# Scatters of edge records paced by the dense part that runs beside them

## Chip, cores and metric

The kernel runs on one core of a Trainium2 chip. The metric is the device time of one execution in microseconds; the median of the timed runs counts. The profile is of one separate execution.

## Reference

Two layers of a graph network, each a graph part and a feed-forward part with residual sums, over N = 6250 nodes of 256 features and E = 100,000 edges:

```python
x = x + L0_gnn(layernorm(x), src, dst, edge_weight, w_self, w_neigh)   # weighted sums of gathered rows, two products, rows divided by their norm
x = x + L0_ffn(layernorm(x), ...)   # shared MLP plus 4 experts, the best 2 weighted
x = x + L1_gnn(layernorm(x), (src, dst), edge_attr_64, ...)
x = x + L1_ffn(layernorm(x), ...)   # 8 experts, the best 2 weighted
...
def L1_gnn(x, edge_index, edge_attr, u, batch, W1, b1, W2, b2):
    src = edge_index[0]
    sums = segment_sum(edge_attr, src, n)          # 64 attributes of each edge, summed by node
    counts = segment_sum(ones, src, n)
    combined = concatenate([x, sums / maximum(counts, 1)[:, None], u[batch]], axis=1)
    return relu(combined @ W1 + b1) @ W2 + b2
```

What matters here is that the second graph part sums 100,000 edge records (64 attributes and two more words, 264 bytes) by source node, for which the kernel first sorts them, and that this sorting needs nothing of the first layer's dense work.

## The kernel before

The nodes lie in 49 tiles of 128 rows, in NG = 7 groups of G = 7 tiles, resident in SBUF. The work has four stages, each a block with one program for each engine; engines meet only at semaphores and at the ends of blocks.

**Gathers.** POOL gathers the normalised source rows of 128 edges with one indirect DMA (L343, 784 of them); ACT multiplies them by the edge weights, TensorE (PE) adds them into tiles by one-hot products, VectorE (DVE) makes the one-hots and adds the results to `acc`. Beside this DVE ranks the edges by source, so that each edge has its place in the sorted list (`pos_i`). At the end of the stage POOL issues the first BEGUN = 16 scatters (L356).

**Dense part and scatters.** This is the stage that the change touches. PE, DVE and ACT go through the 7 groups, each as two chains of 4 and 3 tiles (`CHAINS`) whose steps alternate: the products of the first graph part, the first feed-forward part, and the first product of the second graph part. All of it is written out, without loops on the chip. ACT evicts each product from PSUM: in `ffn` six times at L957 and three at L960, in `part_out` four times at L977; with two chains and seven groups that makes 182 evictions. The first eviction of a group comes after the graph part's products, the squares and norms (L931), a normalisation, the turn of the rows (PE L1078, DVE L1233) and the gate's logits (PE L1092, L1094). The first group can't begin before its weights have landed, which SP loads at the start of the block.

Meanwhile POOL scatters the other 768 columns of 128 edge records to their sorted places in DRAM (`sorted_edges`, L904), one indirect DMA for each column c. The records come through a stage of two halves of SC = 28 columns, which SP refills (L862) once the half's scatters have landed. POOL waits for a half to be loaded, and before every second scatter (EACH = 2) for the landing of the batch that lies two batches back (TURNS = 2). After its scatters POOL has only seven short additions left in this block (L914).

**Edge part.** After the dense part ACT loads the sorted records in 340 items, DVE makes one-hots (L1330), PE multiplies (L1177), DVE adds (L1339). The records are sorted in three segments of columns, and ACT waits before each segment for the landing of its scatters alone:

```python
SEGMENTS = ((0, 448), (448, 672), (672, NC))
...
for n in range(len(SEGMENTS)):
    for turn in range(TURNS):
        act.wait_ge(s_sca[turn], LANDED[n][turn])
    with act.Fori(ITS4_FROM[n], (ITS4_FROM + (ITS4,))[n + 1]) as it:
        loads(it)
```

The segments have 160, 104 and 76 items; the loop goes by 16 items, so the wait for the last segment stands before item 256. The last stage holds the rest of the second layer.

Of the kernel before, what the change touches and what calls it, by code (L numbers as in the profile page):

```python
# [15 lines left out]
NC = -(-E // (P * RUN)) * RUN  # L16
# [91 lines left out]
PHASES = len(CHAINS) * NG  # L108
# [6 lines left out]
EACH = 2  # L115
# [3 lines left out]
BEGUN = 16  # L119
# [3 lines left out]
def build(nc, a, out):  # L123
# [5 lines left out]
    def sem(name):  # L129
        return ctx.enter_context(nc.semaphore(name))  # L130
    def dram(name, shape, dt=f32):
        return nc.dram_tensor(name, shape, dt, kind="Internal").ap()
    with ctx:
# [79 lines left out]
        if True:  # L213
# [66 lines left out]
            with nc.Block() as block:  # L280
                @block.sync
                def _(sp):
                    sp.dma_start(dst_i[:, :], a["dst"].rearrange("(p c) -> p c", p=P)).then_inc(s_dst, 16)
                    sp.dma_start(raw_i[:, 0, :, :], a["src"].rearrange("(j q e) -> q j e", q=QC, e=P)).then_inc(s_cols, 16)
                    for n, (g0, g1) in enumerate(X_PARTS):
                        sp.dma_start(xr[:, g0 * G:g1 * G, :],
                                     a["x"][g0 * G * P:g1 * G * P, :].rearrange("(t p) d -> p t d", p=P)).then_inc(s_x[n], 16)
                    sp.dma_start(raw_i[:, 1, :, :], a["dst"].rearrange("(j q e) -> q j e", q=QC, e=P)).then_inc(s_cols2, 16)
                    sp.dma_start(raw_f[:, 2, :, :], a["w"].rearrange("(j q e) -> q j e", q=QC, e=P)).then_inc(s_cols2, 16)
                    sp.dma_start(src_i[:, :], a["src"].rearrange("(p c) -> p c", p=P)).then_inc(s_src, 16)  # L290
                    for g in range(NG):
                        for h, tiles in enumerate(XN_PARTS):
                            sp.wait_ge(s_xn[h], (g + 1) * len(tiles))
                            first = (g * G + tiles[0]) * P
                            sp.dma_start(xn_d[first:first + len(tiles) * P, :].rearrange("(t p) d -> p t d", p=P),
                                         xn_st[:, tiles[0]:tiles[-1] + 1, :]).then_inc(s_xst[h], 16)
                    sp.wait_ge(s_rank, 1)
                    for h in range(2):
                        sp.dma_start(stage[:, h, :, :], a["attr"].rearrange("(p c) f -> p c f", p=P)[:, h * SC:(h + 1) * SC, :]).then_inc(s_att[h], 16)
                    sp.wait_ge(s_row, 2)  # L300
                    sp.dma_start(item_d.unsqueeze(0), row4_i[:, :, :]).then_inc(s_rst, 16)
                    sp.wait_ge(s_rst, 16)
# [399 lines left out]
        if True:  # L702
# [30 lines left out]
            def nth(c, g):  # L733
                return len(CHAINS) * g + c
            def tiles_to(c, g):
                return G * g + c * len(CHAINS[0])
            def span(c):
                return slice(CHAINS[c][0], CHAINS[c][-1] + 1)
            def columns(c):
                return slice(CHAINS[c][0] * P, (CHAINS[c][-1] + 1) * P)  # L740
# [88 lines left out]
            s_y3 = sem("l0_ffn_products")  # L829
            s_x2 = sem("l0_rows_done")  # L830
            s_hxo = [sem(f"l1_part_out{c}") for c in range(len(CHAINS))]
            with nc.Block() as block:
                @block.sync
                def _(sp):
# [48 lines left out]
                @block.gpsimd  # L883
                def _(pool):
                    own = Chain(pool, s_c3)
                    own.add(pool.iota(rev_i[:, :], pattern=[[-1, 8]], base=8, channel_multiplier=0))
                    own.add(pool.memset(pair[:, :, :], 0.0))
                    own.add(pool.memset(cf[:, :, 4:5], 1.0))
                    own.sync()
                    for m in range(4):  # L890
                        own.add(pool.affine_select(out=pair[:, m // 2, m % 2 * (P // 2):(m % 2 + 1) * (P // 2)],
                                                   in_=pair[:, m // 2, m % 2 * (P // 2):(m % 2 + 1) * (P // 2)],
                                                   compare_op=ALU.not_equal, fill=1.0, base=-m,
                                                   pattern=[[0, P // 2]], channel_multiplier=1))
                    own.sync()
                    for c in range(BEGUN, NC):
                        q, batch = c // SC, c // EACH
                        turn = batch % TURNS
                        if c % SC == 0:
                            pool.wait_ge(s_att[q % 2], (q // 2 + 1) * 16)  # L900
                        if c % EACH == 0:
                            if batch >= TURNS:
                                pool.wait_ge(s_sca[turn], batch // TURNS * (16 * EACH))
                        pool.indirect_dma_start(  # L904
                            out=edges_d, out_offset=bass.IndirectOffsetOnAxis(ap=pos_i[:, c:c + 1], axis=0),
                            in_=stage[:, q % 2, c % SC, :], in_offset=None).then_inc(s_sca[turn], 16)
                    for turn in range(TURNS):
                        pool.wait_ge(s_sca[turn], 16 * EACH * PER_TURN * (NC // SC // 2))
                    for c in range(len(CHAINS)):
                        pool.wait_ge(s_hxo[c], NG * 16)  # L910
                    pool.wait_ge(s_w3, 16 * (18 + 8))
                    for g in range(NG):
                        x = xr[:, g * G:(g + 1) * G, :]
                        pool.tensor_tensor(x, x, gb2[:, :].unsqueeze(1).to_broadcast([P, G, D]), ALU.add).then_inc(s_c5, 1)  # L914
                @block.scalar
                def _(act):
# [18 lines left out]
                    def deviation3(c, g):  # L935
                        act.wait_ge(s_v3, nth(c, g) + 1)
                        nc.scalar.activation(ln["sd"][:, span(c)], ln["mv"][:, span(c), 1], ACT.Sqrt, bias=eps[:, :]).then_inc(s_sd3, 1)
# [8 lines left out]
                    def ffn(c, g):  # L946
                        w = len(CHAINS[c]) * P
                        act.wait_ge(s_mx, nth(c, g) + 1)
                        nc.scalar.activation(gt["e"][:, span(c), :], gt["l"][:, span(c), :], ACT.Exp).then_inc(s_ex, 1)
                        if g:  # L950
                            act.wait_ge(s_hxo[c], g * 16)
                        for m in range(6):
                            if m == 5:
                                act.wait_ge(s_df, nth(c, g) + 1)
                                nc.scalar.activation(g1["x"][:, span(c)], g1["d"][:, span(c)], ACT.Exp).then_inc(s_ex2, 1)
                            act.wait_ge(s_h1, nth(c, g) * 6 + m + 1)
                            nc.scalar.activation(h1[:, m, columns(c)], psum[:, 4 * c + m % 3, 0:w], ACT.Relu, bias=b1[:, m:m + 1]).then_inc(s_h1c, 1)  # L957
                        for m in range(3):
                            act.wait_ge(s_h2, nth(c, g) * 3 + m + 1)
                            nc.scalar.activation(h2[:, m, columns(c)], psum[:, 4 * c + m, 0:w], ACT.Relu, bias=b2[:, m:m + 1]).then_inc(s_h2c, 1)  # L960
                    def deviation4(c, g):
                        act.wait_ge(s_v6, nth(c, g) + 1)
                        nc.scalar.activation(ln["sd"][:, span(c)], ln["mv"][:, span(c), 1], ACT.Sqrt, bias=eps[:, :]).then_inc(s_sd6, 1)
# [7 lines left out]
                    def part_out(c, g, deviation):  # L971
                        w = len(CHAINS[c]) * P
                        for m in range(4):
                            if m == 2 and deviation:
                                deviation3(c, g + 1)
                            act.wait_ge(s_h5, nth(c, g) * 4 + m + 1)
                            nc.scalar.activation(h1[:, m, columns(c)], psum[:, 4 * c + m % 2, 0:w], ACT.Copy).then_inc(s_hc5, 1)  # L977
                        act.wait_ge(s_hc5, nth(c, g) * 4 + 4)
                        act.dma_start(hx_d[g * P:(g + 1) * P, :].rearrange("p (m n) -> p m n", m=4)[:, :, columns(c)],
                                      h1[:, 0:4, columns(c)]).then_inc(s_hxo[c], 16)  # L980
# [1151 lines left out]
```

## Time and profile before

| | us |
|---|---|
| timed runs, median of 3 (lowest, highest) | 3212.76 (3200.77, 3222.05) |
| span of the profiled execution | 4237.5 |
| time of the profiled execution beside its span | not recorded |

The profiled execution is one execution with the recording on; its span runs from its first to its last instruction. It is longer than the timed runs, which are made without it. Busy time of the profiled execution: PE 2615.1 us (62% of the span), DVE 1421.8 (34%), ACT 974.8 (23%), POOL 1860.1 (44%). Times in the rows below are microseconds from the start of the span. "Idle before" is the time that an engine stood still before an instruction, with what ended it: an instruction of another engine, a DMA, "remote" (a semaphore event for which the trace has no source on this core) or "issue" (nothing that the profile shows).

### The profile page before, as it was taken

What the parts mean: (1) busy time and instruction counts of PE and PEld (TensorE: products, weight loads), DVE (VectorE), ACT (ScalarE), POOL (GpSimd) and SP (SyncE); (2) the same over time, 40 slices, a digit from 0 to 9 for tenths busy, and PEclk for the clock granted to TensorE, in tenths of its full rate; (3) what the DMA queues carried; (4) which work ended last, traced back from release to release, by engine and by line L of the source; (5) the groups of instructions that cost most, each with busy time, mean ns of one, the idle gap of its engine ahead of it and who ended that gap; (6) DMA issues with size and microseconds to landing.
All of it is one profiled execution on the core that took longest, in us unless ns stands there. A gap on an engine that the chain in (4) does not pass through costs nothing. (4 is left out here: it accounts for less than half of the span.)

```text
span 4237.5 us, 48325 instructions
## 1 busy us (share of the span) xinstructions
PE 2615.1 (62%) x11859; PEld 2002.8 (47%) x11860; DVE 1421.8 (34%) x3597; ACT 974.8 (23%) x2337; POOL 1860.1 (44%) x1901
## 2 busy tenths in 40 slices
PE   0445545556554221111211699998999879999998
PEld 0333334434443010100100466657996567888898
DVE  5211225666621000000000244438995542222222
ACT  4555222222220000000000244430003421111122
POOL 4566665665665777777777100002000342222222
PEclk9767667676776555555555799999998889999999
DMA  6223333332232111111111000006553454444455
GB/s 187 80 87 91 88 87 97 87 89 80 85 85 62 52 45 51 52 52 62 42 51 42 24 18 18 35 18 172 146 146 116 162 153 110 111 117 116 106 148 148
DMA packets 217917, 372.80 MB, mean 88 GB/s; under 512 B 48901, under 2 KB 146542, under 8 KB 216815
## 3 DMA queue, kind: packets, MB, share of 16 engines
q0 software_dynamic: 82928, 157.51, 14.4%
q1 hardware_dynamic: 77100, 154.03, 11.1%
q10 hardware_dynamic: 57812, 60.35, 5.0%
q8 instruction: 34, 0.56, 0.1%
q14 instruction: 43, 0.35, 0.0%
HBM read 290.03 MB, written 81.71 MB: 88 GB/s over the span
## 5 line engine op out<-in xcount | busy, mean ns | idle before, releaser
L673 PE MATMUL psum<-arena 128*128 x1984 | 632.1, 481 | 514.1 <-issue 325.7
L343 POOL DMA_INDIRECT arena<-xn_rows,arena x784 | 749.7, 956 | 449.7 <-issue 241.9
L904 POOL DMA_INDIRECT sorted_edges<-arena x768 | 766.7, 998 | 284.3 <-issue 265.1
L673 PEld LDWEIGHTS psum<-arena 128*128 128x128 f32 x1984 | 463.3, 243 | 683.1 <-issue 605.6
L408 ACT ACTIVATE arena<-arena 128x256 f32<-128x256 f32 x784 | 338.1, 496 | 697.3 <-DMA arena<-xn_rows,arena 642.6
L1177 PE MATMUL psum<-arena,acc 128*65 128x128 f32 x2720 | 311.9, 275 | 23.8 <-DVE arena L1330 23.8
L1177 PEld LDWEIGHTS psum<-arena,acc 128*65 128x65 f32 x2720 | 296.0, 138 | 40.1 <-DVE arena L1330 32.0
L1103 PE MATMUL psum<-arena 128*128 128x512 f32 (+1 forms) x336 | 172.3, 669 | 229.4 <-ACT arena L957 133.2
L1796 PE MATMUL psum<-arena,xr 128*128 x1344 | 301.7, 382 | 13.7 <-DVE xr L2021 9.1
L1783 PE MATMUL psum<-xr 128*128 128x256 f32 x1344 | 299.1, 381 | 1.0 <-DVE xr L2015 1.0
L575 DVE TENSOR_TENSOR acc<-acc,psum 128x256 f32 x248 | 103.0, 415 | 550.4 <-remote 366.8
L1796 PEld LDWEIGHTS psum<-arena,xr 128*128 128x128 f32 x1344 | 253.8, 192 | 49.1 <-issue 16.0
L1783 PEld LDWEIGHTS psum<-xr 128*128 128x128 f32 x1344 | 256.8, 191 | 36.6 <-DVE xr L2015 1.4
L1330 DVE SCALAR_TENSOR_TENSOR arena<-psum,acc 128x512 f32<-128x512 f32 x340 | 252.5, 744 | 25.2 <-PE psum L1177 15.5
L914 POOL TENSOR_TENSOR xr<-xr,acc 128x1792 f32<-128x1792 f32 x7 | 23.2, 3356 | 516.9 <-DMA acc<-in_f_bg_dram 516.9
L1058 PE MATMUL psum<-arena 128*128 128x256 f32 x392 | 108.7, 427 | 207.0 <-DVE arena L1199 118.2
L1533 POOL DMA_INDIRECT out_y_dram<-xr,acc x84 | 130.9, 1558 | 230.9 <-ACT xr L1651 218.7
L1103 PEld LDWEIGHTS psum<-arena 128*128 128x128 f32 x336 | 74.8, 230 | 315.0 <-issue 157.1
L563 DVE SCALAR_TENSOR_TENSOR arena<-psum,arena 128x512 f32<-128x512 f32 x252 | 188.0, 747 | 88.2 <-issue 80.0
L1058 PEld LDWEIGHTS psum<-arena 128*128 128x128 f32 x392 | 81.0, 216 | 225.1 <-issue 144.3
L1518 POOL DMA_INDIRECT dispatched<-acc,arena x98 | 94.8, 968 | 183.6 <-DVE arena L1915 154.8
L2021 DVE TENSOR_SCALAR xr<-psum,arena 128x256 f32<-128x256 f32 x168 | 73.5, 480 | 243.6 <-PE psum L1783 226.0
(310 smaller groups left out, 3180.9 us busy)
## 6 DMA issues: line engine op xcount, KB each, us to landing
xr<-in_f_W_dram SPq DMA_DIRECT2D x63, 1024.0 KB
acc<-sorted_edges ACTq DMA_DIRECT2D x340, 132.0 KB, 2.2
arena<-in_attr_dram SPq DMA_DIRECT2D x28, 924.0 KB
arena<-xn_rows,arena POOLq DMA_INDIRECT x784
sorted_edges<-arena POOLq DMA_INDIRECT x784
arena<-hidden_parts SPq DMA_DIRECT2D x7, 1792.0 KB, 7.3
arena<-dispatched SPq DMA_DIRECT2D x42, 265.0 KB
arena<-in_f_W_dram SPq DMA_DIRECT2D x8, 1024.0 KB
```

The lines of the kernel that those rows point to most:

```text
L343: pool.indirect_dma_start(out=rows[:, c, :], out_offset=None, in_=xn_d, in_offset=bass.IndirectOffsetOnAxis(ap=idx[:, c:c + 1], axis=0)).t ...
L408: last = nc.scalar.activation(row, row, ACT.Copy, scale=w_c[:, ds((it * SLOTS + u) * RUN + c, 1)])
L563: nc.vector.scalar_tensor_tensor(hot[:, u, :, :], iota_p.unsqueeze(1).to_broadcast([P, RUN, P]), tile_b0[:, ds(i, 1)], dst_c[:, ds((run - ...
L673: last = nc.tensor.matmul(psum[:, bank(u), 0:D], hot[:, u, c, :], rows[:, ds(slots[k] + c, 1), :].squeeze(1), start=c == 0, stop=c == RUN - 1)
L904: pool.indirect_dma_start(out=edges_d, out_offset=bass.IndirectOffsetOnAxis(ap=pos_i[:, c:c + 1], axis=0), in_=stage[:, q % 2, c % SC, :], ...
L1058: last = nc.tensor.matmul(tile_of(c, 2, i), tT[:, i, j, :], (w_self if j < 2 else w_neigh)[:, j % 2, :], start=j == 0, stop=j == 3)
L1103: last = nc.tensor.matmul(psum[:, b + m % 3, 0:w], w1[:, j, m, :], yT[:, j, columns(c)], start=j == 0, stop=j == 1)
L1177: last = nc.tensor.matmul(psum[0:EA + 1, bank4(u), 0:P], rows4[:, u, c, 0:EA + 1], hot4[:, u % RING, c, :], start=c == 0, stop=c == RUN - 1)
L1330: nc.vector.scalar_tensor_tensor(hot4[:, u % RING, :, :], iota4.unsqueeze(1).to_broadcast([P, RUN, P]), tile_b[:, ds(it * STEP4 + u, 1)], ...
L1533: pool.indirect_dma_start(out=out["y"], out_offset=bass.IndirectOffsetOnAxis(ap=wide_meta[:, u, h, 0:1].bitcast(i32), axis=0), in_=wide_y[ ...
L1783: last = nc.tensor.matmul(psum[:, 1 + m // 2, m % 2 * W:(m % 2 + 1) * W], wide_w[:, u, c, m * P:(m + 1) * P], wide_xT[:, c, :], start=c == ...
L1796: last = nc.tensor.matmul(psum[:, 5 + h, 0:D], wide_hT[:, m, h * P:(h + 1) * P], fw2[:, ds(e, 1), m, :].squeeze(1), start=m == 0, stop=m = ...
```

## The change

ACT raises a new semaphore by one after each of the 182 counted evictions. POOL, before each column c that is a multiple of four, waits until that count has reached the share (c - 16) / 768 of 182, rounded down; where that is 0 it doesn't wait. Nothing else changes.

```diff
+            s_step = sem("dense_steps_begun")
+            STEPS = PHASES * (6 + 3 + 4)
+            def steps_before(c):
+                return (c - BEGUN) * STEPS // (NC - BEGUN)
...
                         if c % EACH == 0:
                             if batch >= TURNS:
                                 pool.wait_ge(s_sca[turn], batch // TURNS * (16 * EACH))
+                        if c % (2 * EACH) == 0 and steps_before(c):
+                            pool.wait_ge(s_step, steps_before(c))
                         pool.indirect_dma_start(
...
                             nc.scalar.activation(h1[:, m, columns(c)], psum[:, 4 * c + m % 3, 0:w], ACT.Relu, bias=b1[:, m:m + 1]).then_inc(s_h1c, 1)
+                            act.sem_inc(s_step, 1)
...
                             nc.scalar.activation(h2[:, m, columns(c)], psum[:, 4 * c + m, 0:w], ACT.Relu, bias=b2[:, m:m + 1]).then_inc(s_h2c, 1)
+                            act.sem_inc(s_step, 1)
...
                             nc.scalar.activation(h1[:, m, columns(c)], psum[:, 4 * c + m % 2, 0:w], ACT.Copy).then_inc(s_hc5, 1)
+                            act.sem_inc(s_step, 1)
```

PHASES is 14 (two chains by seven groups), NC 784 and BEGUN 16.

## Rows read from the trace of the kernel before

**Rows 1.** The page's 40 slices of the span: busy tenths of PE and POOL.

```profile
PE   0445545556554221111211699998999879999998
...
POOL 4566665665665777777777100002000342222222
```

**Rows 2.** Windows: stretch, length, busy us (count) by engine, granted clock, DMA.

```profile
1306.00:2357.00 1051.00, 198.75 (x431) 102.19 (x431) 47.13 (x163) 48.35 (x101) 766.66 (x768) 0.54 0.17 52
2397.00:2860.00 463.00, 454.05 (x1790) 287.11 (x1790) 182.64 (x639) 196.19 (x403) 0.00 (x0) 0.96 0.07 24
...
2880.00:3196.00 316.00, 311.88 (x2720) 295.95 (x2720) 297.56 (x679) 0.00 (x0) 16.94 (x6) 0.99 0.54 142
3196.00:4237.00 1041.00, 971.84 (x4773) 823.80 (x4773) 322.06 (x1038) 258.92 (x585) 279.75 (x282) 0.94 0.47 130
```

**Rows 3.** ACT's instructions in order of time, under the scatters: start, duration, idle before.

```profile
1396.81 0.69 ACT L957 ACTIVATE arena<-psum,arena 128x512 f32<-128x512 f32 x1 [11.27 <-issue]
1408.02 0.69 ACT L957 ACTIVATE arena<-psum,arena 128x512 f32<-128x512 f32 x1 [10.52 <-remote]
1418.51 0.69 ACT L957 ACTIVATE arena<-psum,arena 128x512 f32<-128x512 f32 x1 [9.80 <-remote]
```

**Rows 4.** ACT's instructions in order of time, after the last scatter.

```profile
2447.22 0.69 ACT L957 ACTIVATE arena<-psum,arena 128x512 f32<-128x512 f32 x1 [2.84 <-PE psum L1103]
...
2494.57 0.60 ACT L977 ACTIVATE arena<-psum 128x512 f32<-128x512 f32 x1 [0.64 <-PE psum L1149]
...
2505.14 1.03 ACT L957 ACTIVATE arena<-psum,arena 128x384 f32<-128x384 f32 x2
...
2528.70 0.69 ACT L957 ACTIVATE arena<-psum,arena 128x512 f32<-128x512 f32 x1 [2.62 <-PE psum L1103]
2530.78 0.69 ACT L957 ACTIVATE arena<-psum,arena 128x512 f32<-128x512 f32 x1 [1.39 <-PE psum L1103]
...
2779.08 0.69 ACT L957 ACTIVATE arena<-psum,arena 128x512 f32<-128x512 f32 x1 [2.77 <-PE psum L1103]
```

**Rows 5.** Line L977: duration in ns (min/median/max), first and last start.

```profile
L977 ACT ACTIVATE arena<-psum x56: 467/533/598, 1867.2 to 2859.9; 128x512 f32<-128x512 f32 x28, 128x384 f32<-128x384 f32 x28
```

**Rows 6.** Line L343, the gathers: what ended POOL's idle time (us, times).

```profile
  remote: 110.8, 34
  PE psum L673: 74.7, 23
  ACT arena L385: 17.1, 1
```

**Rows 7.** All engines in order of time at the start of the stage.

```profile
1307.66 0.98 POOL L904 DMA_INDIRECT sorted_edges<-arena  x1 [0.30 <-issue]
...
1308.94 0.97 POOL L904 DMA_INDIRECT sorted_edges<-arena  x1 [0.30 <-issue]
...
1313.73 0.97 POOL L904 DMA_INDIRECT sorted_edges<-arena  x1 [2.54 <-DMA sorted_edges<-arena]
...
1317.18 3.55 ACT L925 ACTIVATE arena<-xr,nmr,rstd 128x256 f32<-128x256 f32 x7 [47.49 <-DMA arena<-in_eW_dram]
```

**Rows 8.** Line L904, the scatters: duration, first and last start, a cause of idle time.

```profile
L904 POOL DMA_INDIRECT sorted_edges<-arena x768: 965/971/1796, 1306.4 to 2355.8; - x192
...
  DMA sorted_edges<-arena: 18.7, 12
```

**Rows 9.** Line L1330, DVE's one-hots of the edge part, and its sequencer's steps.

```profile
L1330 DVE SCALAR_TENSOR_TENSOR arena<-psum,acc x340: 739/741/752, 2879.6 to 3193.4; 128x512 f32<-128x512 f32 x170
L1330 DVEq FUSED_REGOPS  x336: 57/57/57, 2881.2 to 3193.0; - x168
```

**Rows 10.** PE's instructions in order of time up to its first L1103.

```profile
1331.50 3.54 PE L1058 MATMUL psum<-arena 128*128 128x256 f32 x8 [4.80 <-DVE arena L1199]
1343.16 1.97 PE L1078 MATMUL psum<-ident,arena 128*128 128x128 f32 x8 [8.12 <-issue]
...
1351.75 7.08 PE L1103 MATMUL psum<-arena 128*128 128x512 f32 x12
```

## Prediction

> **What bounds the kernel now.** I read the page's slices first, and they raise a question before any line does: the recorded span is 4237.5 us, and the median of the timed runs 3212.76 us. The recorded execution is 1025 us longer than what is to be predicted, so the first task is to find what of the trace is not in the timed runs. In the slices [rows 1] PE's digits fall to 1 and 2 in the second quarter of the span while POOL's stand at 6 and 7, and come back to 9 as soon as POOL's are 0. That is the dense part under the scatters, and the dense part without them.
>
> The windows put numbers to it [rows 2]. From 1306 to 2357 POOL issues its 768 scatters and PE is busy 199 us of 1051, at a granted clock of 0.54; from 2397 to 2860, with POOL silent, PE is busy 454 us of 463 at 0.96. The reader should look at what ACT waits for in the first stretch: its evictions at L957 come 10.5 to 11.2 us apart, after idle times put down to "remote" or "issue" [rows 3], where with POOL silent two of them stand 2.1 us apart (2528.70 and 2530.78) [rows 4]. So in the recorded execution the dense part starves while POOL issues.
>
> Its own pace is read where POOL is silent [rows 4]: the first L957 of chain 0 starts at 2447.22 and, one group later, at 2528.70: 81.5 us for a group, which has 26 counted evictions, 3.13 us each. From the last group's first L957 (2779.08) to the last eviction of all at 2859.9 [rows 5] it is 81 us. Seven groups of it take 6 x 81.5 + 81 = 570 us from the first eviction on; the recorded execution took 1463 us for that (1396.8 to 2859.9). Starvation cost it 893 us. The gathers of the stage before lost another 203 us to "remote", PE and ACT [rows 6]. Together 1096 us, and 1025 are to be explained: **most of the starvation cannot be in the timed runs**, or they would be nearer 4200.
>
> What sets the end of a timed run, then? Two paths start at the first scatter, S (1306.4 in the trace [rows 8]), and both end with the last 84 edge items (segment 2, which the loop begins at item 256) and the 1041 us behind them [rows 2].
> - Scatter path: 767 steps of 1.275 us (0.97 and 0.30; starts 1307.66 and 1308.94) [rows 7] = 978 us. The recorded stretch has 71 us more (19 of it waits for landings [rows 8]), so 978 to 1049. Then an estimate of 5 us for the last landing (2.54 us of idle for one [rows 7]) and load, 84 items at 316 / 340 = 0.93 us [rows 2, 9] = 78, and 1041: S + 2102 to 2173.
> - Dense path: 44 us to the first eviction (below), 570, then 20 us to the first item (2859.9 to 2879.6) [rows 5, 9], 316 us for all items and 1041: S + 1991.
>
> The scatter path is longer by 111 us. For S itself: 1306 less 203 of waits is 1103, and 1103 + 2102 = 3205 against 3213 measured. I conclude that **POOL's queue bounds a timed run up to the end of the scatters**, at one indirect DMA per 1.27 us with hardly a wait, and that the dense part hides under it. That is an inference from durations, not something a row shows.
>
> **The change part by part.** It adds 182 increments on ACT (7 x 2 x 13) and 190 waits on POOL: c = 24, 28, ... 780; c = 20 needs 4 x 182 // 768 = 0 steps and has none. Nothing is removed; what moves is the start of scatters, with the 128-row DMA that each issues. Queued behind each waiting scatter are all later ones on POOL, and behind those SP's refills of the attribute stage (L862) and at the end ACT's loads of segment 2.
>
> The waits themselves: POOL's idle time between scatters is 0.30 us throughout, though every second one already has a wait [rows 7, 8]; I put 190 more at 0, at most 190 x 0.057 = 11 us (57 ns is DVE's cheapest sequencer step at L1330 [rows 9], the nearest there is). ACT's 182 increments by the same step are at most 10 us, on the dense path, which has 111 us of cover; if that cover were gone, they would cost those 10.
>
> The wait at the start is the term that counts. By S + 10 POOL has issued c = 16 to 23 and reaches c = 24, which needs one eviction. The dense part has none yet: it waits for its weights until 1317 [rows 7], then goes through the gnn products, the normalisation and the turn. In the trace PE reaches L1103 at 1351.75, 45 us after S [rows 10]; with its own waits of 4.80 and 8.12 us taken out it would be 34, and ACT's first L957 in fact starts at 1396.81, 90 us after S [rows 3]. So the first step comes at S + 34 to S + 90. I take 44, near the PE row, because the 90 contains one of the starved handovers. POOL then waits 44 - 10 = 34 us (24 to 80).
>
> After that the dense part stays ahead. Steps 1 to 9 follow at most 2.1 us apart. Step 10 is the first eviction of part_out, 47.4 us after the first L957 (2494.57 against 2447.22), and c = 60, which needs it, stands 36 scatters or 46 us behind c = 24: 1 us of wait. Step 14 comes after 57.9 us (2505.14), and c = 76 needs it after 66 [rows 4]. From there a step takes the dense part 3.13 us and POOL 768 / 182 x 1.275 = 5.4 us. Sum: 34 + 1 = **35 us on the path**, with nothing to win it back: POOL's pace after the wait is what it was. The timed runs go from 3213 to **3248 us**, bounds 3213 + 24 = 3237 and 3213 + 81 + 11 = 3305. The sum is added to the median because of the recorded execution no time but its span is given, and that span holds the starvation. The recorded span should by contrast go down, since POOL's pauses let the starved handovers through.
>
> By the Trainium skill (NOTIFIC — the notification-queue block, section 7.1), the block that writes trace records holds its producers back inside rather than lose a record, and this can throttle an engine. By that rule the starvation belongs to the recording and the sum stays 3248; without it the first rival below applies. The 1025 us between span and median agree with it, but no run here shows which signal is held.
>
> **The rivals.**
> 1. Faster: part of the starvation is real in timed runs, and the pauses relieve it. The place is PE's signals to ACT and DVE while POOL issues back to back. The price: if the dense path is the longer one now, then with S = 1103 the timed run holds 3213 - 1103 - 1991 = 119 us of starvation, and it can fall to 3094 if all goes; half gives about 3150. It decides only where scatters follow each other closer than (871 / 767 =) 1.14 us, 871 being dense end, 20 and 256 items; otherwise the scatters end later than the dense part needs them. For it: the first slices and "remote" rows. Against: no two scatters in the trace start closer than 0.965 + 0.30 [rows 7, 8].
> 2. The change doesn't bite in time: the dense path is the longer one without starvation that POOL can relieve (the gathers keep half their waits and scatters are quicker unrecorded), and up to 100 us of slack in the scatters swallows the first wait. 3213, give or take 15. For it: unrecorded POOL times are not shown by anything.
> 3. Slower by more: the first evictions come as late as in the trace, 90 us after S, and the tenth step late as well: 3213 + 81 + 11 = 3305. A step of 11 us throughout is excluded: it would keep the dense part behind the scatters to the end, and such a run would by now be as long as the recorded one.
>
> **How the numbers follow.** A measurement of this kernel tells about 1%, 32 us, from no change. The forecast has 0.55, with its own range 3237 to 3265; its centre lies just over the 1% line (3245), so I count 0.34 of it as slower and 0.21 as same. Rival 1 has 0.18 (0.16 faster, 0.02 same), rival 2 has 0.20 (0.15 same, 0.02 faster, 0.03 slower), rival 3 has 0.07, slower. Sum: faster 0.18, same 0.38, slower 0.44. The range runs from 3170, which leaves out the lower part of rival 1 (some 0.12), to 3290, which leaves out the upper part of rival 3 (0.05).
>
> **What would show it.** In the changed kernel's profile: POOL idle at L904 behind ACT for some 30 us or more before the ninth scatter; shorter handovers at L957; scatters stretched out beside the dense part, and a dense part that ends before 2860; a shorter span. If the span falls by hundreds of microseconds and the timed median rises by about 35, both halves of the argument hold. Wrong would be: a timed gain of more than 1% (then the starvation is real in timed runs), or a loss of over 100 us (then POOL waits all along).

## The result, and the profile after

The changed kernel takes 3240.88 us (median of 4 runs, 3239.27 to 3243.92), the kernel before beside it 3214.3 us (median of 4). The ratio is 1.0087, 95% interval 1.0056 to 1.0118: a loss of 28 us, 18 to 38. The forecast was 3248 us, 35 us over before, in a range of 3170 to 3290; the loss falls just inside the 1% that the forecast's three chances called "same".

The profiled execution of the changed kernel has a span of 3239.9 us beside a time of 3241.57 us, so this trace can be laid directly beside the timed runs, as the 4237.5 us of the first trace of the kernel before could not. That time is one of the four timed runs: a recorded execution need not be longer than the timed ones, as the section on the time before says it is. The page's slices, in the form of [rows 1]: PE now stands at 9 and 8 through the dense part while POOL works beside it. Its 1, 0 and 2 come later, where the edge part waits for records that POOL is still scattering.

```profile
PE   0555665666666599999998910929998999999998
...
POOL 4777777777777376777676777671145322322222
```

POOL's instructions in order of time, around the ninth scatter of the block (compare [rows 7]); the scatters' line is L910 in the changed kernel. The first scatter of the block starts at 1089.87, and POOL reaches c = 24 after 1101.8.

```profile
1089.87 0.98 POOL L910 DMA_INDIRECT sorted_edges<-arena  x1 [0.56 <-POOL arena L895]
...
1097.06 0.97 POOL L910 DMA_INDIRECT sorted_edges<-arena  x1 [2.39 <-DMA sorted_edges<-arena]
...
1100.87 0.97 POOL L910 DMA_INDIRECT sorted_edges<-arena  x1 [0.30 <-issue]
1133.76 0.97 POOL L910 DMA_INDIRECT sorted_edges<-arena  x1 [31.92 <-ACTq L964]
1135.03 0.97 POOL L910 DMA_INDIRECT sorted_edges<-arena  x1 [0.30 <-issue]
```

"ACTq L964" is the new increment on ACT's sequencer. What it waited for is ACT's first eviction (L963 in the changed kernel, L957 in [rows 3]), 43 us after the first scatter:

```profile
1132.96 0.69 ACT L963 ACTIVATE arena<-psum,arena 128x512 f32<-128x512 f32 x1 [3.08 <-PE psum L1112]
1135.14 0.69 ACT L963 ACTIVATE arena<-psum,arena 128x512 f32<-128x512 f32 x1 [1.50 <-PE psum L1112]
```

All of POOL's idle time at the scatters, by what ended it (compare [rows 8]):

```profile
L910 POOL DMA_INDIRECT sorted_edges<-arena x768: 962/967/979, 1089.9 to 2174.6; - x192
...
  issue: 232.3, 709
  DMA sorted_edges<-arena: 75.9, 50
  ACTq L964: 34.7, 6
  ACTq L986: 0.6, 2
```

One wait of 31.92 us is nearly all that 190 waits on ACT cost: 35.3 us together, over eight that the trace counts. The next longest that the trace puts down to ACT, 1.58 us at 1680.10, stands before c = 422, which is no multiple of four and has no wait for ACT, so it is not the change's. And the last scatter, at 2174.6, is what the end waits for. DVE's one-hots of the edge part (compare [rows 9]) stand idle 219.9 us for records, in two waits:

```profile
L1339 DVE SCALAR_TENSOR_TENSOR arena<-psum,acc x340: 735/741/753, 1723.8 to 2256.7; 128x512 f32<-128x512 f32 x170
...
  DMA acc<-sorted_edges: 219.9, 2
```

The windows, in the form of [rows 2], divided at the first eviction, the last eviction, the last scatter and the last edge item:

```profile
1134.00:1710.00 576.00, 562.79 (x2218) 355.52 (x2216) 227.62 (x787) 243.07 (x500) 406.56 (x421) 0.96 0.22 71
1710.00:2176.00 466.00, 235.13 (x2049) 225.08 (x2048) 229.20 (x511) 0.49 (x1) 327.58 (x339) 0.76 0.46 130
2176.00:2260.00 84.00, 77.64 (x672) 74.93 (x672) 74.69 (x172) 0.00 (x0) 23.24 (x7) 0.95 0.52 136
2260.00:3239.00 979.00, 944.36 (x4773) 812.75 (x4773) 320.64 (x1037) 256.88 (x585) 279.12 (x282) 0.98 0.50 139
```

In the first of them PE is busy 563 of 576 us at a granted clock of 0.96, with POOL at work beside it. After the dense part PE is busy half of the 466 us until the last scatter; 84 us for the last items and 979 us for the rest follow.

### The profile page after: what moved, and what is told of

It reads as the page before. It is cut to its first block and busy times, and to the rows that moved or that the text cites. A ratio compares the mean times of both kernels' runs of the same rounds, so it can differ in the third digit from the quotient of the medians.

```text
span 3239.9 us, 48670 instructions
## 1 busy us (share of the span) xinstructions
PE 2472.3 (76%) x11859; PEld 1954.9 (60%) x11860; DVE 1421.5 (44%) x3597; ACT 964.6 (30%) x2337; POOL 1832.2 (57%) x1901
## 5 line engine op out<-in xcount | busy, mean ns | idle before, releaser
L910 POOL DMA_INDIRECT sorted_edges<-arena x768 | 742.1, 966 | 344.1 <-issue 232.3
L343 POOL DMA_INDIRECT arena<-xn_rows,arena x784 | 747.1, 953 | 250.8 <-issue 225.5
L673 PE MATMUL psum<-arena 128*128 x1984 | 609.8, 471 | 345.9 <-ACT arena L408 317.7
L673 PEld LDWEIGHTS psum<-arena 128*128 128x128 f32 x1984 | 455.4, 237 | 500.2 <-issue 421.3
L1339 DVE SCALAR_TENSOR_TENSOR arena<-psum,acc 128x512 f32<-128x512 f32 x340 | 252.4, 743 | 238.6 <-DMA acc<-sorted_edges 219.9
L1805 PEld LDWEIGHTS psum<-arena,xr 128*128 128x128 f32 x1344 | 253.3, 191 | 35.3 <-issue 2.4
L1602 ACT ACTIVATE arena<-ident,rcount 128x128 f32<-128x128 f32 x49 | 15.0, 390 | 557.7 <-PEq L836 553.8
L1112 PE MATMUL psum<-arena 128*128 128x512 f32 (+1 forms) x336 | 148.8, 604 | 0.0
L1660 ACT ACTIVATE xr<-xr,acc 128x256 f32<-128x256 f32 x84 | 42.6, 508 | 348.5 <-DVE xr L2036 348.5
L2036 DVE TENSOR_TENSOR xr<-psum,acc 128x256 f32<-128x256 f32 x84 | 35.6, 424 | 218.9 <-PE psum L1805 218.9
L1537 POOL COPY acc<-acc 128x18 f32<-128x18 f32 x43 | 8.6, 199 | 207.3 <-DVE xr L2024 201.0
```

Source lines behind the costliest of these rows:

```text
L343: pool.indirect_dma_start(out=rows[:, c, :], out_offset=None, in_=xn_d, in_offset=bass.IndirectOffsetOnAxis(ap=idx[:, c:c + 1], axis=0)).t ...
L673: last = nc.tensor.matmul(psum[:, bank(u), 0:D], hot[:, u, c, :], rows[:, ds(slots[k] + c, 1), :].squeeze(1), start=c == 0, stop=c == RUN - 1)
L910: pool.indirect_dma_start(out=edges_d, out_offset=bass.IndirectOffsetOnAxis(ap=pos_i[:, c:c + 1], axis=0), in_=stage[:, q % 2, c % SC, :], ...
L1112: last = nc.tensor.matmul(psum[:, b + m % 3, 0:w], w1[:, j, m, :], yT[:, j, columns(c)], start=j == 0, stop=j == 1)
L1339: nc.vector.scalar_tensor_tensor(hot4[:, u % RING, :, :], iota4.unsqueeze(1).to_broadcast([P, RUN, P]), tile_b[:, ds(it * STEP4 + u, 1)], ...
L1805: last = nc.tensor.matmul(psum[:, 5 + h, 0:D], wide_hT[:, m, h * P:(h + 1) * P], fw2[:, ds(e, 1), m, :].squeeze(1), start=m == 0, stop=m = ...
```

## The experiments

There are ten experiments, in three groups, each timed beside the kernel before on the same chip. The theory is that of the prediction: POOL's queue bounds the run up to the end of the scatters, and the change costs the wait for the first eviction. The rivals are many small costs, and a starvation of the dense part that is real in timed runs.

**The kernel before, recorded a second time.** No edit.

> The kernel before, unchanged, for a second profile of it. Theory A (the starvation of its first profile came with that one recorded execution and is not in the timed runs): ratio 1.00, and every span that a run lists lies within some 15 us of its time, near 3213. Theory B (recording always starves the dense part of the unpaced kernel): timed ratio 1.00, but the profiled span again some 1000 us over the median. Theory C (part of it is in timed runs): spans of the runs scattered by over 2%.

Measured: ratio 1.0008 (0.9992 to 1.0025), span of the profiled execution 3197.0 us beside a time of 3198.71. Its slices, its scatters, its first eviction and DVE's waits for records:

```profile
PE   0555656666666499999997931929998999999998
...
POOL 4777777777777676777777777680155222322222
```

```profile
L904 POOL DMA_INDIRECT sorted_edges<-arena x768: 962/967/1011, 1088.6 to 2131.2; - x192
...
  DMA sorted_edges<-arena: 75.6, 59
```

```profile
1131.34 0.69 ACT L957 ACTIVATE arena<-psum,arena 128x512 f32<-128x512 f32 x1 [3.08 <-PE psum L1103]
1133.46 0.69 ACT L957 ACTIVATE arena<-psum,arena 128x512 f32<-128x512 f32 x1 [1.43 <-PE psum L1103]
```

```profile
L1330 DVE SCALAR_TENSOR_TENSOR arena<-psum,acc x340: 734/740/752, 1720.9 to 2213.7; 128x512 f32<-128x512 f32 x170
...
  DMA acc<-sorted_edges: 179.3, 3
```

The first eviction comes 42.7 us after the first scatter and the next 2.1 us later, with POOL issuing all the while: no starvation, without any pacing. Each of the ten timed runs lists a span of its own, 1.66 to 1.75 us under its time. Theories B and C fall. The first trace shows one exceptional execution. From here this trace stands for the kernel before.

**Increments alone.** The three `act.sem_inc(s_step, 1)` stay, POOL's wait goes.

```diff
-                        if c % (2 * EACH) == 0 and steps_before(c):
-                            pool.wait_ge(s_step, steps_before(c))
```

> ACT's 182 increments alone; POOL waits for none of them. Theory (the loss is POOL's first wait): no loss, 3214 us, ratio 0.997 to 1.003; the dense part under the scatters takes no more than 5 us longer. Rival (the increments on ACT cost the time): the loss of 27 us stays, 3241.

Measured: ratio 1.001 (0.9993 to 1.0027), 3206.95 us beside 3202.06; its scatters run from 1089.8 to 2129.0, as before, and its last eviction starts at 1705.4 (1708.4 before). The increments cost nothing that can be measured.

**The waits without the first.** POOL waits from step 23 on (c = 116); the first 23 of the 190 waits are left out.

```diff
-                        if c % (2 * EACH) == 0 and steps_before(c):
+                        if c % (2 * EACH) == 0 and steps_before(c) > 22:
```

> The change without its waits up to step 22: POOL waits from c = 116 on alone (167 waits of 190). Theory (the first wait is all of the loss, and behind it the dense part is always ahead): no wait on ACT over 1 us in the trace, ratio 0.997 to 1.003 against before, 3214 us. Rival (190 waits each cost a little, or the pacing slows the scatters as a whole): the loss stays in proportion, 20 us or more, 3234 to 3241.

Measured: ratio 1.0001 (0.9982 to 1.0019). The trace puts 2.9 us (four times) and 2.0 us (six times) of POOL's idle time down to ACT's increments, with the usual 0.30 us of each in them. One of them is longer than the 1 us that was expected at most: 1.74 us at 1677.01. It stands before c = 450, which has no wait for ACT, and the second trace of the kernel before has 1.41 us for a landing at the same scatter. These 167 waits cost nothing that can be measured, within 6 us.

**The first wait alone.**

```diff
-                        if c % (2 * EACH) == 0 and steps_before(c):
-                            pool.wait_ge(s_step, steps_before(c))
+                        if c == 24:
+                            pool.wait_ge(s_step, steps_before(c))
```

> Of the change's 190 waits only the one at c = 24, for one eviction. Theory: the whole loss, 25 to 32 us, 3239 to 3246, with one POOL idle time of 32 us before the ninth scatter of the block. Rival (many small waits): under 10 us, 3214 to 3224.

Measured: ratio 1.0109 (1.0086 to 1.0132), a loss of 35 us (28 to 42; 25 to 32 was expected), and in the trace one idle time for ACT:

```profile
1133.44 0.97 POOL L910 DMA_INDIRECT sorted_edges<-arena  x1 [31.21 <-ACTq L964]
```

With the run before it: 167 waits for nothing, one for the whole loss. The other 22 (c = 28 to 112) were not run alone; with them, in the full change, the loss is no larger.

**A longer first wait.** Only c = 24 waits, for ten evictions in place of one.

```diff
-                        if c % (2 * EACH) == 0 and steps_before(c):
-                            pool.wait_ge(s_step, steps_before(c))
+                        if c == 24:
+                            pool.wait_ge(s_step, 10)
```

> One wait alone, at c = 24, for ten evictions in place of one. The tenth comes 90 us after the first scatter of the block, and the eight scatters before it take some 11 us. Theory (POOL's queue bounds the run up to the end of the scatters, so each microsecond of POOL's wait is one of the run): POOL waits some 79 us, the run takes 79 us more than before, 3280 us, ratio 1.025; DVE's wait for the last segment's records grows from some 110 to 190 us. Rival (part of a wait is absorbed by slack): under 60 us, ratio under 1.019.

Measured: ratio 1.026 (1.0232 to 1.0288), a loss of 83 us (74 to 92). POOL's wait:

```profile
1180.45 0.96 POOL L910 DMA_INDIRECT sorted_edges<-arena  x1 [78.21 <-ACTq L986]
```

78 us of wait for 83 us of time: microsecond for microsecond, within the interval. DVE's waits came otherwise than expected. They sum to 222.7 us here, 43 more than in the kernel before, and the wait for the last segment's records didn't grow at all (63.46 us, 64.50 before); the one for the second segment did, from 114.65 to 159.27. The rest stands ahead of the first record, where the trace calls it "issue":

```profile
L1339 DVE SCALAR_TENSOR_TENSOR arena<-psum,acc x340: 735/741/752, 1768.1 to 2304.0; 128x512 f32<-128x512 f32 x170
...
  DMA acc<-sorted_edges: 222.7, 2
```

```profile
1768.12 3.38 DVE L1339 SCALAR_TENSOR_TENSOR arena<-psum,acc 128x512 f32<-128x512 f32 x5 [46.43 <-issue]
```

The last eviction in this trace is at 1710.0, but the first segment's last scatter (c = 447) starts only at 1759.9, in the kernel before at 1672.1: so late the first segment waits for POOL as well, which the expectation had left out. The two parts, 43 and 46 us, together make 89, and the last scatter starts 90 us later than in the kernel before:

```profile
L910 POOL DMA_INDIRECT sorted_edges<-arena x768: 962/967/977, 1089.8 to 2221.6; - x192
...
  DMA sorted_edges<-arena: 86.3, 62
```

**The change once more,** on the chip of the longer wait.

> The change itself, unaltered, on the chip of these runs. Theory: it loses the first wait's 32 us and nothing more, ratio 1.008 to 1.011, as the one wait at c = 24 did alone (1.0109). Rival (the other 189 waits cost or gain something): a ratio outside 1.005 to 1.014.

Measured: ratio 1.0089 (1.0056 to 1.0122). What the trace puts down to ACT is 31.7 us (three times), 0.6 us (twice) and 0.3 us (once); its waits for landings are 76.7 us.

**Fewer waits for landings.** If POOL's queue is the bound, its 76 us of waits for landings are on the path. They stand behind batches of two scatters, each batch waiting for the one two back (`TURNS = 2`).

```diff
-TURNS = 2
+TURNS = 4
```

> The kernel before with TURNS = 4 in place of 2: POOL waits before a batch for the landing of the batch four back, not two back. Its 76 us of waits for landings should shrink to under 20, and the end of the scatters come 55 to 75 us sooner; slack on the dense path is 110 us, so all of it should show: 3130 to 3150 us, ratio 0.977 to 0.983. Rival (the DMA queue takes no more scatters and POOL stands still in another place): ratio 0.997 to 1.003.

Measured: 3143.72 us, ratio 0.9787 (0.9766 to 0.9808), a gain of 68 us (62 to 75). The idle time for landings is nearly gone, and the last scatter comes 66 us sooner than in the kernel before:

```profile
L904 POOL DMA_INDIRECT sorted_edges<-arena x768: 963/967/977, 1089.6 to 2064.8; - x192
...
  issue: 227.5, 746
  DMA sorted_edges<-arena: 6.4, 21
```

This beats both kernels, and DVE still waits 107.6 us for records, so the dense part is not the longer path here either. 767 steps in 975.2 us are 1.271 us each, which is the pace of the instruction itself with its 0.30 us between.

**TURNS = 4 with the late waits.** The two edits above together.

> TURNS = 4 with the change's waits from step 23 on alone. If the scatters run faster, the pacing is nearer to binding: scatters need a step every 5.4 us and the dense part makes one every 3.1, so still no wait of a microsecond or more after the first group; as the kernel before with TURNS = 4, within 0.4%. Rival (paced waits begin to bind): slower than that by 10 us or more.

Measured: ratio 0.977 (0.9744 to 0.9796), no different from TURNS = 4 alone.

**TURNS = 4 with the full change.**

> The change in full, with TURNS = 4. Theory: the first wait costs its 32 us as before, so 32 to 40 us over TURNS = 4 alone: 3170 to 3185 us, ratio 0.988 to 0.993. The scatters come 70 us sooner than with TURNS = 2, but a step every 5.4 us is still slower than the dense part's 3.1, so no second wait over 5 us. Rival (with the landings out of the way the pacing binds in more places): over 45 us on TURNS = 4 alone.

Measured: 3168.29 us, ratio 0.9884 (0.9866 to 0.9902). By the ratios that is 31 us over TURNS = 4 alone (0.9787, on another chip; 32 to 40 was expected), and by the medians 34 us over the next kernel, which ran on the same chip. The trace puts 35.9 us (six times), 2.7 (six) and 1.8 (six) of POOL's idle time down to ACT's increments. In the first sum is the wait at c = 24, 34.33 us; the one other that stands out is at c = 60, which needs the tenth step:

```profile
1179.82 0.97 POOL L910 DMA_INDIRECT sorted_edges<-arena  x1 [1.17 <-ACTq L986]
```

The wait costs as much with the landings out of the way, and beyond c = 60 no wait for ACT stands out.

**TURNS = 4 and four more scatters ahead of the block.**

```diff
-BEGUN = 16
+BEGUN = 20
```

> The kernel before with TURNS = 4, and BEGUN = 20 in place of 16: four more scatters go out in the block of the gathers, where POOL stands idle for 5.6 us at the block's end. Theory (POOL's queue still bounds the run with TURNS = 4): 5 us less than TURNS = 4 alone, 3130 to 3140 us, ratio 0.974 to 0.979. Rival (the dense path bounds by now, or the block's end comes later by as much): no gain on TURNS = 4, or a loss of up to 5 us.

Measured: 3134.71 us, ratio 0.979 (0.977 to 0.981), beside 0.9787 for TURNS = 4 alone. Intervals of 6 us to either side can't tell a gain of 5 us from none, but the trace can: the last scatter starts at 2064.3, where TURNS = 4 alone has 2064.8. POOL in order of time shows where the gain went:

```profile
1085.46 0.97 POOL L356 DMA_INDIRECT sorted_edges<-arena  x1 [0.30 <-issue]
1092.32 0.14 POOL L886 IOTA arena<- 128x8 int32 x1 [5.90 <-POOLq L280]
...
1094.29 0.98 POOL L904 DMA_INDIRECT sorted_edges<-arena  x1 [0.37 <-POOL arena L891]
```

POOL's last scatter ahead of the block starts 5.4 us later than in the kernel before (1080.10), and the next block begins later by as much (IOTA at 1092.32 against 1086.64). The idle time of 5.58 us at the block's end is still there (5.90) though POOL comes to it later, so it was not one that more work on POOL could fill.

## Why the prediction was right

**The bound.** Two paths were worked out from the first trace: scatters S + 2102 to 2173, dense part S + 1991. In the second trace of the kernel before S is 1088.6 (1103 was taken, with all waits of the gathers removed), the scatters take 1042.6 us (978 to 1049 was the span of the bounds), and the span ends 2108 us after S. The longer wait and TURNS = 4 show the bound from both sides: 78 us more of POOL's wait make the run 83 us longer, 69 us less make it 68 us shorter.

The prediction's own ground for the bound was weaker than it looked. It had POOL issue "at one indirect DMA per 1.27 us with hardly a wait", because 1103 + 2102 = 3205 came so near the 3213 measured. That nearness was luck, from errors that cancel: S was 14 us too late, the scatters at their bare pace are 65 us too short, and the 1041 us behind the edge part, read in the first trace, are 979 in the trace after. POOL does wait: 75.6 us for landings in the second trace of the kernel before, 69.5 to 86.3 in every later trace with TURNS = 2, where the first trace had 18.7 [rows 8]. The forecast of the change doesn't depend on this, since S, the scatters and the end are the same with and without it; the gain from TURNS = 4 does. The cover of the dense part was worked out at 111 us, with the scatters at their bare pace; DVE's waits for records put it at 179 us.

**The dense part's own pace.** 44 us to the first eviction and 570 from there were taken, 614 us from S; the trace after has 43.1 and 577 (last eviction at 1710.2, 620.3 us after S). Reading it where POOL was silent gave the right figure for the place where POOL is not. The 44 was in part luck: it was put near PE's first L1103, 45 us after S in the first trace, but the eviction comes behind that product. In the second trace of the kernel before L1103 starts 38.9 us after S and the eviction 3.8 us later. The lower bound of 34 took PE's wait of 8.12 us out as starvation, and the second trace has 7.99 us at the same place, for ACT's L943, so that wait belongs to the path; and 45 less 4.80 and 8.12 is 32, not 34.

**The first wait.** 34 us were taken, from 44 less 10. Measured 31.9: the eight scatters ahead of it took 12 us and not 10, since one of them waited 2.39 us for a landing, as in [rows 7]. The trace of before had the row; I left it out of the sum. With TURNS = 4, where no landing is waited for there, the wait is 34.33 us.

**The tenth step.** 1 us was taken; with TURNS = 2 it does not show, since c = 60 waits longer for a landing. With TURNS = 4 it does: 1.17 us idle, 0.87 more than the usual 0.30.

**The small terms.** 190 waits and 182 increments were put at nothing. It is shown for the increments (1.001 alone) and for 167 of the waits (1.0001); for the 22 between them and the first it follows only from the full change losing no more than c = 24 alone (1.0087 and 1.0089 against 1.0109).

**The sum.** 35 us forecast, 28 measured (18 to 38), 35 (28 to 42) for the first wait alone, 29 (18 to 39) for the change once more. By the interval the forecast's loss holds; which side of 1% the change lies on the runs don't settle.

**What failed: the reading of the first trace.** The prediction concluded rightly that the starvation was not in the timed runs, but went on to say that the changed kernel's span would go down "since POOL's pauses let the starved handovers through". The span went down, and not for that: the kernel before, recorded again, has no starvation either (3197.0 us). So "both halves of the argument", which the prediction would have taken as proven by a shorter span and a longer time, were not proven by them; only the second profile of before told. The Trainium skill (NOTIFIC — the notification-queue block, section 7.1) was cited for recording that holds an engine back; recording alone doesn't do it here, since eleven more executions were profiled and none starved. What made the first one starve stays open; it did not come again. Late handovers were not all of it: ACT stood 40.93 us before one instruction (L949, at 1385.33) that the trace has waiting for nothing.

**The rivals.** A relief of real starvation (3094 to 3150) and a dense path that hides the wait (3213) both needed the dense path to be the longer one; it is shorter, as DVE's idle time for records shows (179.3 us in the second trace of the kernel before). A larger loss from a first eviction at S + 90 rested on the exceptional execution.

## What to carry to other kernels

When a span and the timed median differ by a third, ask first which stage of the trace can't have been there, and take a second profile of the same kernel before reading anything into the first. A wait put on the engine whose queue bounds the stage cost its length here, and the one that cost was the first, where the engine to be followed hadn't started; a count compared with a share says little until one asks when the first count comes. The same bound shows where to gain: on POOL's path it was the depth of the scatter queue, two batches against four, worth 2%.

## What had not been expected of the hardware

Of twelve profiled executions (the kernel before and the change twice each, eight edited kernels once) one, the first of the kernel before, ran 1025 us longer than the timed runs, with ACT's evictions 10.5 to 11.2 us apart while POOL issued [rows 3]; in a later recording the same code has its first two 2.1 us apart. And scatters that wait only for the batch four back run at 1.271 us a scatter, the bare pace of the instruction, where waiting for the batch two back puts 69 us more of waits into 768 of them.
